# Attention: a pair's shift transposed once as 32 rows and laid into the query stack by two transfers on the chip

## The chip, the cores and the metric

The kernel runs on one NeuronCore of a Trainium2 chip. Its engines run beside each other and meet at semaphores: TensorE (PE: matmuls and transposes, results into PSUM), VectorE (DVE), ScalarE (ACT), GpSimd (POOL) and SyncE (SP, which issues DMA transfers here). The metric is the device time of one execution in microseconds (us).

## What is computed

Four layers on a stream `x` of 2 x 2048 tokens with 256 channels: linear attention, a mixture of experts, softmax attention on a hyperboloid, and a second mixture of experts. The change lies in the third one:

```python
x = L0_attn_x
x = x + _L0_attn_ref(_layernorm(x, axis=-1), ...)
x = x + _L0_ffn_ref(_layernorm(x, axis=-1), ...)
x = x + _L1_attn_ref(_layernorm(x, axis=-1), ...)
x = x + _L1_ffn_ref(_layernorm(x, axis=-1), ...)

# in _L1_attn_ref: B = 2, T = 2048, h = 16 heads of dh = 16
sc = (-jnp.einsum('bhqi,bhki->bhqk', q[..., :1], k[..., :1]) + jnp.einsum('bhqc,bhkc->bhqk', q[..., 1:], k[..., 1:])) / dh ** 0.5
at = jax.nn.softmax(sc, axis=-1)
out = jnp.einsum('bhqk,bhkc->bhqc', at, vv)
```

## The kernel before

The stages stand one behind the other with a barrier between them. Softmax attention is the stage `at` (function `attention`, tiles named `at_...`). It works on 16 pairs of heads (`NPAIR`: 8 pairs in each of 2 batches). The queries of a pair lie in `k.QT` (rows of `l1c_QT` in the profile): 64 partitions for each of the two heads, 2048 columns, one for each query, in float16. Keys lie in `k.KT` in the same way. A pair takes `ST` = 32 steps. A step is half of one key tile: two units of 128 keys x 1024 columns (512 queries of each head).

What sets the order is the order in which each engine's instructions are written, with waits on counting semaphores. There is no scheduler. In one step:

- PE does `scores(p, step, 0)` (L1581, two matmuls), `weigh` of the step two back (L1595, eight matmuls as the trace counts a step: each float32 one is recorded in two passes), `scores(p, step, 1)`, and one `means` (L1608).
- ACT does one exponential of 128 x 1024 for each unit (L1681), from `psS` into `pexp`. `psS` has two buffers, so `scores` of a unit waits until the exponential of two units before is done (`raised`).
- DVE takes the maximum of what `means` wrote (L1695), one for each step.

Softmax needs a shift for each query, so that the exponentials stay in range. The kernel estimates it: `means` multiplies the queries with sums of four keys, `reduce` takes the row maximum into a column of `mx`, and six steps ahead of the next pair all 32 columns are there (16 query tiles x 2 heads). `make_shift` (L1713 to L1716) turns `mx` into `shift`, 128 partitions x 32 float16. The shift must then lie along the columns of the query stack, as row `ROW` = 32 of each head's 64 partitions, where a constant key row picks it up in `scores`. That turn is done in two halves of 8 tiles, at steps 27 and 29 (`TURNS`):

- `turn_shift` (L1632) on PE: 16 transposes of one column each, 128x1 into 1x128, eight for each head, into `psX`;
- `put_shift` (L1723) on DVE: two copies of 1 x 1024 (one for each head) from `psX` into `k.QT`, then a count on `x_free`, which hands `psX` on.

PE waits for all four copies (`q_ready`) ahead of the pair's first `scores`. `psX` is one bank; the results of the pair before go through it too, at steps 3 and 5 (`turn_out`, L1640, four float32 transposes of 128x128, and `divide`, L1738 to L1742, on DVE). The dictionary `x_use` numbers these uses.

Ahead of the loop stands a prologue for pair 0: `first_means` (L1620) and `first_reduce` (L1700) for 16 tiles and 3 more, `make_shift(0)`, and both halves of the turn. The last pair has no successor and needs neither `means` nor a shift, so there are 15 turned shifts inside the loop and one in the prologue. From step 26 of the last but one pair (pair 14) on there are no `means` either.

Of the kernel before, what the change touches and what calls it, by code (L numbers as in the profile page):

```python
# [23 lines left out]
P = 128  # L24
# [1464 lines left out]
def attention(nc, k):  # L1489
# [17 lines left out]
    AHEAD = 6  # L1507
    TURNS = (ST - 5, ST - 3)
    with Stage(nc, "at") as s:
# [4 lines left out]
        sa, sb_ = s.sb("sa", [P, ST]), s.sb("sb", [P, ST])  # L1514
        shift = s.sb("shift", [P, ST, 1], F16)
        oT = s.sb("oT", [P, 2, BANK])
# [4 lines left out]
        psX = s.ps("psX", [P, BANK])  # L1521
        (scored, raised, weighed, v_ready, o_out, maxed, reduced, k_ready, q_ready, shifted, x_turned, x_free, chain,
         divided, start) = (
            s.sem(n) for n in ("scored", "raised", "weighed", "vready", "oout", "maxed", "reduced", "kready", "qready",
                               "shifted", "xturned", "xfree", "chain", "divided", "start"))

        def uses():
            order = [("shift", 0, 0), ("shift", 0, 1)]
            for p in range(NPAIR):
                if p:  # L1530
                    order += [("out", p - 1, 0), ("out", p - 1, 1)]
                if p + 1 < NPAIR:
                    order += [("shift", p + 1, 0), ("shift", p + 1, 1)]
            return {u: n for n, u in enumerate(order + [("out", NPAIR - 1, 0), ("out", NPAIR - 1, 1)])}
# [17 lines left out]
        with nc.Block() as block:  # L1552

            @block.gpsimd
            def _(pool):
# [11 lines left out]
                for p in range(2, NPAIR):  # L1567

                    pool.wait_ge(weighed, 6 + (p - 1) * ST * 2)
                    take_v(p)  # L1570

            @block.tensor
            def _(pe):
# [48 lines left out]

                def turn_shift(p, half):
                    pe.wait_ge(shifted, p + 1)
                    use = x_use["shift", p, half]
                    if use:
                        pe.wait_ge(x_free, use)
                    view = psX[:, :].bitcast(F16)
                    for hh in range(2):
                        row = hh * HR + ROW  # L1630
                        for n in range(KT16 // 2):
                            mm = pe.transpose(view[row:row + 1, n * P:(n + 1) * P],  # L1632
                                              shift[:, (half * (KT16 // 2) + n) * 2 + hh, :], k.identh[:, :])
                    mm.then_inc(x_turned, 1)

# [10 lines left out]
                for t in range(AHEAD // 2):  # L1646
                    first_means(1, t)
                for half in range(2):
                    turn_shift(0, half)

                pe.wait_ge(reduced, ST + AHEAD)
                for p in range(NPAIR):
                    pe.wait_ge(q_ready, 4 * (p + 1))
                    for step in range(ST):
                        scores(p, step, 0)
                        if step >= 2:
                            weigh(p, step - 2)
                        elif p:
                            weigh(p - 1, ST - 2 + step)
                        scores(p, step, 1)  # L1660
                        q, n = mean_at(p, step)
                        if q < NPAIR:
                            means(q, n)
                        if step in (3, 5) and p:
                            turn_out(p - 1, step // 4)
                        if step in TURNS and p + 1 < NPAIR:
                            turn_shift(p + 1, TURNS.index(step))
                weigh(NPAIR - 1, ST - 2)
# [16 lines left out]
            def _(dve):  # L1685
# [21 lines left out]
                def make_shift(p):  # L1707
                    dve.wait_ge(reduced, (p + 1) * ST)
                    if p:

                        dve.wait_ge(x_turned, x_use["shift", p - 1, 1] + 1)
                    q = 0.25 / (QS * QS)
                    link(p, 0, dve.tensor_scalar(sa[:, :], mx[:, :], q, 280.0, ALU.mult, ALU.add))  # L1713
                    link(p, 1, dve.tensor_scalar(sa[:, :], sa[:, :], -280.0, None, ALU.min))
                    link(p, 2, dve.scalar_tensor_tensor(sb_[:, :], mx[:, :], q, sa[:, :], ALU.mult, ALU.max))
                    dve.tensor_scalar(shift[:, :, 0], sb_[:, :], -QS * QS / KONE, None, ALU.mult).then_inc(shifted, 1)  # L1716

                def put_shift(p, half):
                    use = x_use["shift", p, half]
                    dve.wait_ge(x_turned, use + 1)  # L1720
                    for hh in range(2):
                        row = hh * HR + ROW
                        dve.tensor_copy(keys(k.QT, p)[row:row + 1, half * UN:(half + 1) * UN],  # L1723
                                        psX[:, :].bitcast(F16)[row:row + 1, :]).then_inc(q_ready, 1)
                    dve.wait_ge(q_ready, 4 * p + 2 * half + 2)
                    dve.sem_inc(x_free, 1)

# [25 lines left out]
                for t in range(AHEAD // 2):  # L1753
                    first_reduce(1, t)
                put_shift(0, 0)
                put_shift(0, 1)
                for p in range(NPAIR):
                    for step in range(ST):
# [10 lines left out]
                        if step in (3, 5) and p:  # L1769
                            divide(p - 1, step // 4)  # L1770
                        if step in TURNS and p + 1 < NPAIR:
                            put_shift(p + 1, TURNS.index(step))
                for y in range(2):
# [440 lines left out]
```

## Time and profile before

| | |
|---|---|
| median of 3 runs | 2600.14 us |
| lowest and highest | 2599.54, 2600.92 us |
| the profiled execution | 2600.85 us, its span 2599.0 us |
| mean granted TensorE clock | 0.938 |
| PE, DVE, ACT, POOL busy | 2240.9, 1263.2, 1492.3, 383.1 us |

Times in the profile count from the span's start. The attention stage runs in it from about 755 to 1790 us. An instruction's duration runs from its start to its end, and the next of the same engine may begin before that end. So the rate of an engine is read from the distance of two starts, called pitch below, and not from the durations. A row of the timeline gathers instructions of one kind as long as no idle time of 0.15 us or more lies between them; its second column runs from the first start to the last end.

### The profile page before, as it was taken

How to read it: one execution, taken by the hardware profiler on the slowest of the kernel's cores; microseconds unless marked ns; L12 is line 12 of the kernel's file. 1: busy time of each engine (PE TensorE's matmuls, PEld its weight loads, DVE VectorE, ACT ScalarE, POOL GpSimd, SP SyncE). 2: the span in 40 equal slices, each digit the busy share in tenths (PEclk: the TensorE clock that was granted, in tenths of full speed). 3: DMA queues.
4: the chain of work that ended last, by engine and by line, in shares of the span. 5: the costliest groups of instructions: out<-in, count | busy, mean ns of one | idle time of the engine just before them, and what ended most of it. 6: DMA issues, size and time to landing. Idle time of an engine off the chain costs nothing. (4 is left out here: it accounts for less than half of the span.)

```text
span 2599.0 us, 41169 instructions
## 1 busy us (share of the span) xinstructions
PE 2240.9 (86%) x12824; PEld 1055.9 (41%) x12825; DVE 1263.2 (49%) x2727; ACT 1492.3 (57%) x2466; POOL 383.1 (15%) x628
## 2 busy tenths in 40 slices
PE   4996799933979999999999999999057999999993
PEld 3783455522642222222222222225034666666662
DVE  5566522246884444444444444421465444444444
ACT  2213433224748999999999999997553222222220
POOL 0030266641000000000000000000001222222220
PEclk9998899976988999999999999999578999999996
DMA  5001122241100000000000000003263444344445
GB/s 180 1 1 65 45 77 79 75 176 69 34 9 1 1 1 1 1 1 1 1 1 1 1 1 1 1 1 115 80 183 99 119 119 119 119 120 120 120 116 211
DMA packets 105458, 160.19 MB, mean 62 GB/s; under 512 B 9465, under 2 KB 81905, under 8 KB 105329
## 3 DMA queue, kind: packets, MB, share of 16 engines
q1 hardware_dynamic: 90544, 117.05, 14.8%
q0 software_dynamic: 13632, 37.24, 4.4%
q10 hardware_dynamic: 1152, 4.19, 0.4%
q8 instruction: 79, 1.29, 0.2%
q14 instruction: 51, 0.41, 0.1%
HBM read 118.86 MB, written 35.39 MB: 59 GB/s over the span
## 5 line engine op out<-in xcount | busy, mean ns | idle before, releaser
L1681 ACT ACTIVATE at_pexp<-at_psS 128x1024 f32<-128x1024 f32 x1024 | 968.0, 1023 | 59.8 <-PE at_psS L1581 56.8
L1695 DVE TENSOR_REDUCE at_mx<-at_psM 128x1 f32<-128x512 f32 x474 | 327.4, 691 | 478.3 <-PE at_psM L1608 478.3
L1595 PE MATMUL at_psO<-at_pexp,at_vst 128*32 128x512 f32 x4096 | 546.4, 605 | 0.1
L1581 PE MATMUL at_psS<-l1c_QT,l1c_KT 64*128 64x512 f16 x2048 | 403.9, 387 | 12.2 <-ACT at_pexp L1681 6.1
L1581 PEld LDWEIGHTS at_psS<-l1c_QT,l1c_KT 64*128 64x128 f16 x2048 | 100.4, 92 | 617.0 <-ACT at_pexp L1681 556.0
L2008 PE MATMUL ex_psH<-wide_wgu,ex_xT 128*128 x852 | 339.9, 549 | 0.1
L2052 ACT ACTIVATE ex_sg<-ex_bias 128x228 f32<-128x228 f32 x213 | 83.7, 393 | 288.1 <-DVE ex_bias L2078 255.1
L2078 DVE TENSOR_TENSOR ex_bias<-ex_psH,ex_bias 128x456 f32<-128x456 f32 x213 | 134.7, 633 | 198.4 <-PE ex_psH L2008 192.9
L2008 PEld LDWEIGHTS ex_psH<-wide_wgu,ex_xT 128*128 128x128 f32 x852 | 157.2, 191 | 138.5 <-issue 138.4
L1005 POOL DMA_INDIRECT expert_rows<-ex_y,ex_odx x142 | 140.4, 989 | 397.4 <-issue 286.0
L2031 PE MATMUL ex_psY<-wide_w2b,ex_hT 114*128 (+1 forms) x852 | 196.0, 379 | 0.7 <-DVE ex_y L2097 0.7
L1608 PE MATMUL at_psM<-at_ksumT,l1c_QT 64*128 64x512 bf16 x474 | 179.1, 378 | 0.7
L2031 PEld LDWEIGHTS ex_psY<-wide_w2b,ex_hT 114*128 114x128 f32 (+1 forms) x852 | 156.3, 190 | 19.8 <-issue 1.3
L999 POOL DMA_INDIRECT ex_xg<-normed,ex_idx x142 | 139.7, 983 | 112.0 <-POOL ex_odx L990 53.5
L1061 PE MATMUL ex_psH<-l_w,ex_xT 128*128 x284 | 141.3, 621 | 5.6 <-issue 2.2
L1557 POOL COPY at_vst<-wide_x 128x512 f32<-128x512 f32 x16 | 9.7, 609 | 898.5 <-PE at_psO L1595 898.5
L1595 PEld LDWEIGHTS at_psO<-at_pexp,at_vst 128*32 128x32 f32 x4096 | 80.6, 108 | 130.2 <-issue 122.9
L1122 DVE TENSOR_SCALAR ex_y<-ex_psY,top_wgt 128x256 f32<-128x256 f32 x71 | 34.3, 483 | 176.6 <-DMA expert_rows<-ex_y,ex_odx 105.8
L2044 ACT ACTIVATE ex_xT<-ex_psX 128x256 f32<-128x256 f32 x71 | 27.2, 384 | 157.1 <-PE ex_psX L1997 157.1
L1099 ACT ACTIVATE ex_hT<-ex_psG 128x256 f32<-128x256 f32 x71 | 27.3, 384 | 131.6 <-PE ex_psG L1070 79.0
L985 POOL CAST ex_idx<-top_tok 128x1 uint32 (+1 forms) x142 | 28.6, 201 | 428.2 <-POOLq L74 420.4
L2083 DVE TENSOR_TENSOR ex_h<-ex_bias,ex_sg 128x228 f32<-128x228 f32 x213 | 82.8, 389 | 11.2 <-ACT ex_sg L2052 11.2
(337 smaller groups left out, 2631.5 us busy)
## 6 DMA issues: line engine op xcount, KB each, us to landing
ex_bias<-in_L_ffn_bg SPq DMA_DIRECT2D x71, 342.0 KB
ex_bias<-in_L_ffn_b SPq DMA_DIRECT2D x71, 342.0 KB
normed<-rt_area SPq DMA_DIRECT2D x16, 512.0 KB, 2.6
lm_y<-expert_rows SPq DMA_DIRECT2D x16, 512.0 KB
cb_y<-expert_rows SPq DMA_DIRECT2D x16, 512.0 KB, 7.6
w_raw<-in_L_ffn_w SPq DMA_DIRECT2D x24, 256.0 KB
wide_wgu<-in_L_ffn_Wg SPq DMA_DIRECT2D x8, 684.0 KB
wide_wgu<-in_L_ffn_W SPq DMA_DIRECT2D x8, 684.0 KB
```

Source lines behind the costliest of these rows:

```text
L999: pool.indirect_dma_start(xg[:, g, :], None, k.xn_d, bass.IndirectOffsetOnAxis(idx[:, g, :], 0)).then_inc(got[g], 16)
L1005: pool.indirect_dma_start(k.y_d, bass.IndirectOffsetOnAxis(odx[:, j, :], 0), y[:, j, :], None).then_inc(put[j], 16)
L1061: mm = pe.matmul(psH[:, j, :], xT[:, j, kk, :], k.w13[:, ds(e, 1), kk, :].rearrange("p a c -> p (a c)"), start=(kk == 0), stop=(kk == KC - 1))
L1581: mm = pe.matmul(psS[:, n, hh * BANK:(hh + 1) * BANK], keys(k.KT, p)[r, kt * P:(kt + 1) * P], keys(k.QT, p)[r, c * BANK:(c + 1) * BANK], s ...
L1595: mm = pe.matmul(psO[g * VW:(g + 1) * VW, y, :], vst[:, p % 2, hh, kt, :], pexp[:, (p * ST + step) % 3 * 2 + n, hh * BANK:(hh + 1) * BANK] ...
L1608: pe.matmul(psM[:, :], keys(k.QT, p)[r, t * P:(t + 1) * P], ksumT[r, p % 2, :], start=True, stop=True).then_inc(maxed, 1)
L1681: act.activation(pexp[:, u % 6, :], psS[:, u % 2, :], ACT.Exp, scale=D ** -0.5 / (QS * QS)).then_inc(raised, 1)
L1695: dve.tensor_reduce(mx[:, n:n + 1], psM[:, :], AX.X, ALU.max).then_inc(reduced, 1)
L2008: mm = pe.matmul(psH[:, n, 0:G2].rearrange("p (n c) -> p n c", n=2), xT[:, j, kk, :], k.wgu[:, ds(e, 1), kk, :, n * HW:(n + 1) * HW].rearr ...
L2031: mm = pe.matmul(psY[:, 0:C], hT[0:rows, j, g, :], k.w2b[0:rows, ds(e, 1), g, :].rearrange("p a c -> p (a c)"), start=(g == 0), stop=(g == ...
L2052: act.activation(sg[:, n, :], bias[:, st.slot(1, BR), n, 0, :], ACT.Silu).then_inc(gated, 1)
L2078: dve.tensor_tensor(hb, psH[:, n, 0:G2].rearrange("p (n c) -> p n c", n=2), hb, ALU.add).then_inc(added, 1)
```

## The change

`shift` is laid out head by head (`[P, 2, KT16]`), and the turn is one transpose of the whole tile: 128x32 in, 32x128 out, at one place, step 28 (`TURN`). DVE copies these 32 rows of 128 from `psX` into a new SBUF tile `shiftT`. Then SP, which had nothing to do in this stage, issues two DMA transfers from SBUF to SBUF for each pair: 16 rows of `shiftT` (256 bytes each) become one row of 2048 columns in `k.QT`. PE waits for both transfers (`shift_in`) ahead of the pair's first `scores`. Before it writes `shiftT` again, DVE waits for the transfers of the pair before. A pair's shift is now one use of `psX` instead of two.

```diff
-    TURNS = (ST - 5, ST - 3)
+    TURN = ST - 4
-        shift = s.sb("shift", [P, ST, 1], F16)
+        shift = s.sb("shift", [P, 2, KT16], F16)
+        shiftT = s.sb("shiftT", [ST, P], F16)
...
+            @block.sync
+            def _(sp):
+                for p in range(NPAIR):
+                    sp.wait_ge(x_free, x_use["shift", p, 0] + 1)
+                    for hh in range(2):
+                        row = hh * HR + ROW
+                        sp.dma_start(keys(k.QT, p)[row:row + 1, :].rearrange("a (t c) -> a t c", c=P),
+                                     shiftT[hh * KT16:(hh + 1) * KT16, :]).then_inc(shift_in, 16)
...
-                def turn_shift(p, half):
+                def turn_shift(p):
                     pe.wait_ge(shifted, p + 1)
-                    use = x_use["shift", p, half]
+                    use = x_use["shift", p, 0]
                     if use:
                         pe.wait_ge(x_free, use)
-                    view = psX[:, :].bitcast(F16)
-                    for hh in range(2):
-                        row = hh * HR + ROW
-                        for n in range(KT16 // 2):
-                            mm = pe.transpose(view[row:row + 1, n * P:(n + 1) * P],
-                                              shift[:, (half * (KT16 // 2) + n) * 2 + hh, :], k.identh[:, :])
-                    mm.then_inc(x_turned, 1)
+                    pe.transpose(psX[:, :].bitcast(F16)[0:ST, 0:P], shift[:, :, :].rearrange("p h t -> p (h t)"),
+                                 k.identh[:, :]).then_inc(x_turned, 1)
...
-                for half in range(2):
-                    turn_shift(0, half)
+                turn_shift(0)
...
-                    pe.wait_ge(q_ready, 4 * (p + 1))
+                    pe.wait_ge(shift_in, 32 * (p + 1))
...
-                        if step in TURNS and p + 1 < NPAIR:
-                            turn_shift(p + 1, TURNS.index(step))
+                        if step == TURN and p + 1 < NPAIR:
+                            turn_shift(p + 1)
...
-                    dve.tensor_scalar(shift[:, :, 0], sb_[:, :], -QS * QS / KONE, None, ALU.mult).then_inc(shifted, 1)
-
-                def put_shift(p, half):
-                    use = x_use["shift", p, half]
-                    dve.wait_ge(x_turned, use + 1)
-                    for hh in range(2):
-                        row = hh * HR + ROW
-                        dve.tensor_copy(keys(k.QT, p)[row:row + 1, half * UN:(half + 1) * UN],
-                                        psX[:, :].bitcast(F16)[row:row + 1, :]).then_inc(q_ready, 1)
-                    dve.wait_ge(q_ready, 4 * p + 2 * half + 2)
-                    dve.sem_inc(x_free, 1)
+                    dve.tensor_scalar(shift[:, :, :].rearrange("p h t -> p t h"),
+                                      sb_[:, :].rearrange("p (t h) -> p t h", h=2), -QS * QS / KONE, None, ALU.mult).then_inc(shifted, 1)
+
+                def put_shift(p):
+                    dve.wait_ge(x_turned, x_use["shift", p, 0] + 1)
+                    if p:
+
+                        dve.wait_ge(shift_in, 32 * p)
+                    dve.tensor_copy(shiftT[:, :], psX[:, :].bitcast(F16)[0:ST, 0:P]).then_inc(x_free, 1)
...
-                put_shift(0, 0)
-                put_shift(0, 1)
+                put_shift(0)
...
-                        if step in TURNS and p + 1 < NPAIR:
-                            put_shift(p + 1, TURNS.index(step))
+                        if step == TURN and p + 1 < NPAIR:
+                            put_shift(p + 1)
```

On PE, at steps 27 to 29 of pair 0, the program before stands thus (L1581 is `scores`, L1595 `weigh`, L1608 `means`, L1632 the turn):

```order
L1608 MATMUL at_psM<-at_ksumT,l1c_QT 128x512
L1632 MATMUL at_psX<-top_identh,at_shift 1x128 x16
L1581 MATMUL at_psS<-l1c_QT,l1c_KT 128x512 x2
L1595 MATMUL at_psO<-at_pexp,at_vst 32x512 x4
L1581 MATMUL at_psS<-l1c_QT,l1c_KT 128x512 x2
L1608 MATMUL at_psM<-at_ksumT,l1c_QT 128x512
L1581 MATMUL at_psS<-l1c_QT,l1c_KT 128x512 x2
L1595 MATMUL at_psO<-at_pexp,at_vst 32x512 x4
L1581 MATMUL at_psS<-l1c_QT,l1c_KT 128x512 x2
L1608 MATMUL at_psM<-at_ksumT,l1c_QT 128x512
L1632 MATMUL at_psX<-top_identh,at_shift 1x128 x16
```

On the same engine at step 28, the changed program (its lines are L1591, L1605, L1618, and L1638 for the turn):

```order
L1591 MATMUL at_psS<-l1c_QT,l1c_KT 128x512 x2
L1605 MATMUL at_psO<-at_pexp,at_vst 32x512 x4
L1591 MATMUL at_psS<-l1c_QT,l1c_KT 128x512 x2
L1618 MATMUL at_psM<-at_ksumT,l1c_QT 128x512
L1638 MATMUL at_psX<-top_identh,at_shift 32x128
L1591 MATMUL at_psS<-l1c_QT,l1c_KT 128x512 x2
```

Two blocks of 16 transposes, behind the `means` of steps 27 and 29, have become one transpose behind that of step 28.

On DVE, from the shift of the next pair on, before (L1695 is `reduce`, L1716 the end of `make_shift`, L1723 `put_shift`, L1733 `take_out`):

```order
L1716 TENSOR_SCALAR at_shift<-at_sb 128x32
L1695 TENSOR_REDUCE at_mx<-at_psM 128x1 x2
L1723 COPY l1c_QT<-at_psX 1x1024 x2
L1695 TENSOR_REDUCE at_mx<-at_psM 128x1 x2
L1723 COPY l1c_QT<-at_psX 1x1024 x2
L1695 TENSOR_REDUCE at_mx<-at_psM 128x1 x3
L1733 COPY at_oT<-at_psO 128x512 x2
```

And in the changed program, at the same place on DVE:

```order
L1720 TENSOR_SCALAR at_shift<-at_sb 128x16x2
L1699 TENSOR_REDUCE at_mx<-at_psM 128x1 x3
L1728 COPY at_shiftT<-at_psX 32x128
L1699 TENSOR_REDUCE at_mx<-at_psM 128x1 x4
L1735 COPY at_oT<-at_psO 128x512 x2
```

Four copies of one partition each have become one copy of 32 partitions, and what brought the row into `k.QT` now stands on SP.

## Rows read from the trace of the kernel before

**Rows 1.** The page: span, busy times, and the granted TensorE clock in 40 slices
```profile
span 2599.0 us, 41169 instructions
...
PE 2240.9 (86%) x12824; PEld 1055.9 (41%) x12825; DVE 1263.2 (49%) x2727; ACT 1492.3 (57%) x2466; POOL 383.1 (15%) x628
...
PEclk9998899976988999999999999999578999999996
```

**Rows 2.** Waits, 800 to 1780 us: waiter, awaited: us in total, times, longest
```profile
PEld at_psS L1581 <- ACT at_pexp L1681: 546.4, 820, 0.8
...
ACT at_pexp L1681 <- PE at_psS L1581: 23.8, 87, 0.3
```

**Rows 3.** Timeline of ACT: start, us covered, instructions xcount, [idle before <- releaser]
```profile
862.87 40.41 ACT L1681 ACTIVATE at_pexp<-at_psS 128x1024 f32<-128x1024 f32 x43 [0.29 <-PE at_psS L1581]
903.57 1.02 ACT L1681 ACTIVATE at_pexp<-at_psS 128x1024 f32<-128x1024 f32 x1 [0.28 <-PE at_psS L1581]
904.88 2.85 ACT L1681 ACTIVATE at_pexp<-at_psS 128x1024 f32<-128x1024 f32 x3 [0.29 <-PE at_psS L1581]
907.93 1.02 ACT L1681 ACTIVATE at_pexp<-at_psS 128x1024 f32<-128x1024 f32 x1 [0.19 <-PE at_psS L1581]
909.25 11.56 ACT L1681 ACTIVATE at_pexp<-at_psS 128x1024 f32<-128x1024 f32 x12 [0.29 <-PE at_psS L1581]
...
925.29 40.42 ACT L1681 ACTIVATE at_pexp<-at_psS 128x1024 f32<-128x1024 f32 x43 [0.29 <-PE at_psS L1581]
...
1674.27 41.37 ACT L1681 ACTIVATE at_pexp<-at_psS 128x1024 f32<-128x1024 f32 x44 [0.29 <-PE at_psS L1581]
...
1719.87 11.35 ACT L1681 ACTIVATE at_pexp<-at_psS 128x1024 f32<-128x1024 f32 x12 [0.17 <-PE at_psS L1581]
1731.51 51.53 ACT L1681 ACTIVATE at_pexp<-at_psS 128x1024 f32<-128x1024 f32 x55 [0.29 <-PE at_psS L1581]
```

**Rows 4.** Timeline of PE around the first turn of one pair (step 27)
```profile
902.06 0.38 PE L1608 MATMUL at_psM<-at_ksumT,l1c_QT 64*128 64x512 bf16 x1
902.37 0.83 PE L1632 MATMUL at_psX<-top_identh,at_shift 128*1 128x128 f16 x16
903.13 0.39 PE L1581 MATMUL at_psS<-l1c_QT,l1c_KT 64*128 64x512 f16 x2
903.45 1.07 PE L1595 MATMUL at_psO<-at_pexp,at_vst 128*32 128x512 f32 x8
...
905.20 1.07 PE L1595 MATMUL at_psO<-at_pexp,at_vst 128*32 128x512 f32 x8
```

**Rows 5.** Timeline of DVE in the same step
```profile
902.48 0.69 DVE L1695 TENSOR_REDUCE at_mx<-at_psM 128x1 f32<-128x512 f32 x1 [1.22 <-PE at_psM L1608]
```

**Rows 6.** Timelines of DVE, PE and ACT at the end of the prologue
```profile
781.80 1.41 DVE L1723 COPY l1c_QT<-at_psX 1x1024 f16<-1x1024 f16 x2
784.85 1.41 DVE L1723 COPY l1c_QT<-at_psX 1x1024 f16<-1x1024 f16 x2 [1.64 <-PE at_psX L1632]
```
```profile
783.41 1.40 PE L1632 MATMUL at_psX<-top_identh,at_shift 128*1 128x128 f16 x16 [3.58 <-DVEq L1726]
786.36 1.04 PE L1581 MATMUL at_psS<-l1c_QT,l1c_KT 64*128 64x512 f16 x4 [1.55 <-issue]
```
```profile
787.01 4.69 ACT L1681 ACTIVATE at_pexp<-at_psS 128x1024 f32<-128x1024 f32 x5 [31.76 <-PE at_psS L1581]
```

**Rows 7.** Windows: stretch, us, busy us (x) of PE, PEld, DVE, ACT, POOL, clock, DMA share, GB/s
```profile
792.00:793.00 1.00, 1.00 (x8) 0.28 (x5) 0.00 (x0) 0.03 (x1) 0.00 (x0) 0.50 0.05 16
793.00:794.00 1.00, 1.00 (x11) 0.16 (x8) 0.69 (x1) 1.00 (x2) 0.00 (x0) 0.97 0.00 0
```

**Rows 8.** SP's transfers of L1361 (SBUF to SBUF) and L1143: issue ns, landing us
```profile
L1361 SPq DMA_DIRECT2D sh_v<-wide_x x32: 485/486/601, 622.8 to 725.3; - x32
...
DMA to landing us min/median/max: 2.0/2.0/2.1
```
```profile
DMA to landing us min/median/max: 3.8/7.6/12.7
```

More of the change, by code:

```diff
@@ L1521, in attention @@
         psX = s.ps("psX", [P, BANK])
-        (scored, raised, weighed, v_ready, o_out, maxed, reduced, k_ready, q_ready, shifted, x_turned, x_free, chain,
+        (scored, raised, weighed, v_ready, o_out, maxed, reduced, k_ready, shift_in, shifted, x_turned, x_free, chain,
          divided, start) = (
-            s.sem(n) for n in ("scored", "raised", "weighed", "vready", "oout", "maxed", "reduced", "kready", "qready",
+            s.sem(n) for n in ("scored", "raised", "weighed", "vready", "oout", "maxed", "reduced", "kready", "shiftin",
                                "shifted", "xturned", "xfree", "chain", "divided", "start"))
         def uses():
-            order = [("shift", 0, 0), ("shift", 0, 1)]
+            order = [("shift", 0, 0)]
             for p in range(NPAIR):
@@ L1532, in uses @@
                 if p + 1 < NPAIR:
-                    order += [("shift", p + 1, 0), ("shift", p + 1, 1)]
+                    order += [("shift", p + 1, 0)]
             return {u: n for n, u in enumerate(order + [("out", NPAIR - 1, 0), ("out", NPAIR - 1, 1)])}
@@ L1709, in make_shift @@
                     if p:
-                        dve.wait_ge(x_turned, x_use["shift", p - 1, 1] + 1)
+                        dve.wait_ge(x_turned, x_use["shift", p - 1, 0] + 1)
                     q = 0.25 / (QS * QS)
```

## The prediction

> **What bounds the kernel now.** The page comes first, only to place the stage: the span is 2599.0 us, and the clock row reads 9 in every slice of the attention loop [rows 1]. The page's busy shares don't say what limits that loop, so the waits of 800 to 1780 us are read next. PE's weight loads of `scores` waited 820 times for the exponential, 546.4 us in total, while ACT waited 87 times for `scores`, 23.8 us in total and never over 0.3 us [rows 2]. So the exponentials on ACT set the pace, and PE is late only at few places. A gain has to come out of these 87 places, from the prologue, or not at all.
>
> The timeline of ACT shows where they are [rows 3]. In the last pair, which turns nothing behind step 5, 55 exponentials cover 51.53 us: a pitch of (51.53 - 1.02) / 54 = 0.935 us. In an ordinary pair 43 of them cover 40.41 us, a pitch of (40.41 - 1.02) / 42 = 0.938. That is the undisturbed pace, 1.87 us for a step of two. Then come four gaps in a row, ahead of 903.57, 904.88, 907.93 and 909.25, and two more up to 925.29. The first four stand behind the two turns of the shift, at steps 27 and 29; the other two stand behind `turn_out`. The whole repeats from 862.87 to 925.29, 62.42 us for 64 exponentials, and every pair from 1 to 13 has the same picture.
>
> **What the turns cost now.** From 862.87 to 909.25 there are 43 + 1 + 3 + 1 = 48 exponentials in 46.38 us [rows 3]. At 0.938 they would take 45.01, so the two turns cost 1.37 us on the path. A little of it is paid back: behind a gap ACT runs at (2.85 - 1.02) / 2 = 0.915 for three pitches [rows 3], which gives back 3 x 0.023 = 0.07. That leaves 1.30 for a pair. Fourteen of the fifteen turned shifts in the loop are of this kind (those made in pairs 0 to 13): 14 x 1.30 = 18.2 us. In pair 14, without `means` in its last steps, 44 + 4 = 48 exponentials run from 1674.27 to 1719.87, 45.60 us, so 0.59 lost. Together 18.8 us.
>
> The timeline of PE says why a turn costs what it does [rows 4]. The `means` starts at 902.06, the 16 transposes at 902.37, and the next `scores` at 903.13. Without a turn, when PE is behind and works without waiting, the distance from one `weigh` to the next is 905.20 - 903.45 = 1.75 us; of it 0.32 lies between `scores` and `weigh` (903.13 to 903.45), 1.00 in `weigh`, and the rest, 0.43, in the second `scores` and `means`, about half each. So some 0.20 us pass from `means` to the next `scores` without a turn, and 1.07 with one: a turn takes 0.87 us of PE. The step has 1.87 - 1.75 = 0.12 us of slack, and two turns, 1.74 us of PE, cost ACT 1.30: each turn has 0.22 absorbed, from this step and the next.
>
> **What the change removes and adds on PE.** Out go 32 transposes and one of two turns for each pair, in comes one transpose of 32 columns. The 16 transposes cover 0.83 us, and one of them lasts about 0.22, so their pitch is 0.61 / 15 = 0.04 and they make 0.65 of the 0.87; the other 0.22 are the waits and the change from one kind of matmul to another. The new turn is then 0.22 + 0.04 = 0.26 us of PE, against 0.22 absorbed: 0.04 us lost, times 15 gives 0.6 us. No row shows a transpose with 32 weight columns in this place. The bounds are nothing (all absorbed) and the cost of `turn_out`, four transposes of full width in float32: from 909.25 to 925.29 there are 16 exponentials in 16.04 us against 15.01, so 1.03 for two, 0.5 each [rows 3], or 7.5 us for 15. The new turn has one short float16 transpose and not four, so it is near the lower end; I take 0.6 us.
>
> **DVE.** Four copies of 0.7 us each (two of them in 1.41) [rows 6] go, one copy of 128 columns comes. DVE had waited 1.22 us ahead of `reduce` [rows 5], and no ACT gap is traced to it, so this is worth nothing by itself. The new wait for `x_turned` stands behind the `reduce` of step 28, which takes 0.69 us; the transpose is done by then. The wait for the transfers of the pair before is one whole pair old. Behind both stand only the `reduce` of step 29 and what follows, which `means` needs a step later.
>
> **SP and the two transfers.** SP has no other work in this stage, so nothing is queued behind its wait. What counts is whether the row lies in `k.QT` when PE starts the next pair. Put onto an undisturbed step with the times of rows 4 and 5: `reduce` ends at 902.48 + 0.69 = 903.17, the copy at about 903.4 (an estimate, from 0.69 for 512 columns), the first issue comes at 903.5. An issue occupies SP for 0.49 us and a transfer from SBUF to SBUF lands 2.0 us after its issue [rows 8], so the second lands at 903.5 + 0.5 + 2.0 = 906.0. The next pair's first `scores` is due three steps behind the `scores` that would follow at about 902.37: 902.37 + 3 x 1.87 = 907.98. There are 2.0 us to spare, and inside the loop the transfers cost nothing. The row's transfer is 128 KB in 1 KB pieces, the new one 4 KB in pieces of 256 bytes. I take the row's 2.0 us. Bounds are about the same 2.0 and the 7.6 us of a transfer of 512 KB from HBM [rows 8].
>
> The page "DMA: Bandwidth & Descriptors" of the Trainium skill, section Specifications, puts the least size for full rate at 512 bytes and says that below it the engine reads, modifies and writes. No row here has such a transfer by itself; by this rule the pieces would be slower than the row's, and if that doubled the whole 2.0 us, the loop would still hide it.
>
> **The prologue.** Here the shift is on the path from its making to the first `scores`. Before, DVE is held by `first_reduce` until 781.80, copies until 783.2, waits for the second half's transposes (PE at 783.41, because `psX` was taken), copies from 784.85 to 786.26, and PE starts at 786.36 [rows 6]. After: the copy from 781.80 to about 782.0, the first issue at 782.1, the second at 782.6, its landing at 784.6, PE at 784.7. That is 1.7 us sooner. But PE runs at a granted clock of 0.50 there, the level of 1.2 GHz, and goes to 2.4 GHz only at 793.0 [rows 7]. If the rise stays at that moment instead of moving with the work, 1.7 us more of the loop run at half clock, where PE sets the pace, and up to half of the gain, 0.85 us, is lost. Between 0.85 and 1.7 I take 1.3 us.
>
> **The sum.** 18.8 + 1.3 - 0.6 = 19.5 us less. The profiled execution took 2600.85 us, so it would become 2581.3. That execution is 0.7 above the median of 2600.14, and the median would become 2580.6. Everything behind the loop starts behind a barrier and moves along whole; its low-clock stretches (the 5, 7 and 8 behind the loop in the clock row [rows 1]) can fall a little differently against the work, for which I allow 2 us either way.
>
> **The rivals.**
>
> *The turn stays dear.* The fixed share of a turn, 0.22 by the split above, might be larger with another shape of weights, so that one turn costs ACT what a `turn_out` does, 0.5 us. Then 7.5 us go instead of 0.6, and the time is 2587.5. For it: the split of 0.87 rests on differences of 0.1 us. Against it: both kinds of turn cost about in proportion to the PE time they take. 8 in 100.
>
> *Small pieces are slow.* A landing after 4.0 us instead of 2.0 costs nothing in the loop (2.0 to spare) and 2.0 in the prologue: 2582.6. 6 in 100.
>
> *The transfers come too late, slower than before.* The place is PE's wait for `shift_in` at each pair's start; behind it stand `scores`, and so ACT. The price is the landing beyond 4.0 us, for each of 15 pairs. At 5.3 us the 1.3 us gained for a pair are gone, and from there on the kernel is slower. At the 7.6 us of a large load [rows 8] it would be 15 x 3.6 = 54 us in the loop and 5.6 in the prologue against 19.5: about 2640. Against it: no other transfer of the program is under way in this stage, and the row's transfers landed within 2.0 to 2.1 us. 4 in 100.
>
> *The change doesn't do what it says.* The four gaps would come from steps 27 to 30 themselves, not from the turn, and the time would stay near 2599. Against it: pair 15 has no turn there and no gap [rows 3]. 2 in 100.
>
> *The part behind the loop moves by more than 2 us*, in either direction, by the clock: 4 in 100.
>
> **How the numbers follow.** The forecast has 76 in 100 and lies between 2578 and 2583. With the slow pieces (2582.6) and the new turn's cost somewhat up its range, 2577.5 to 2585.5 leaves less than 2 in 10 out: the dear turn, the late transfers, the change without effect. A difference of 0.2% (5.2 us) is about what a measurement of this kernel can tell from none. Faster by more than that: the forecast, the dear turn, the slow pieces and most of the clock case, 0.94. Within it: the change without effect, 0.02. Slower: the late transfers, 0.04.
>
> **What would show it.** In the changed kernel's ACT timeline the four gaps at each pair's end are gone, one group of some 55 exponentials runs on from step 5 or so to the next pair's start at a pitch of 0.938, and a pair takes 61.1 us instead of 62.42. On PE, 0.25 us or so at most lie between `means` and `scores` of step 28 beyond the usual. Landing of the new transfers reads about 2 us, and PE has no wait for them but in the prologue, where the first exponential starts near 785.3 instead of 787.01. I am wrong if a new gap stands at each pair's start (late transfers), if a gap of 0.3 us stays at step 28 (the turn stays dear), or if the stage gets shorter and the rest longer.

## The result, and the profile after

The changed kernel takes 2579.19 us (median of 6 runs, 2577.47 to 2581.85), against 2600.53 for the kernel before in the same comparison. The ratio is 0.9919, with an interval of 0.9906 to 0.9932: 0.8% faster, 21.3 us. Forecast were 2580.6, and 19.5 us less. The profiled execution has a span of 2578.4 us, 20.6 less than before.

From the page of the changed kernel: span, busy times, and the granted clock in 40 slices, as in [rows 1].

```profile
span 2578.4 us, 40128 instructions
...
PE 2220.9 (86%) x12328; PEld 1033.4 (40%) x12329; DVE 1223.7 (47%) x2679; ACT 1488.6 (58%) x2466; POOL 382.7 (15%) x628
...
PEclk9998899976988999999999999999588999999996
```

DVE lost 40 us of busy time and PE 20, and the span 20.6. That the second pair of numbers agrees is no proof of a cause; the timeline of ACT has to show where the 20.6 lie. It stands here from the start of the attention loop on, in the columns of [rows 3] (the line of the exponential is now L1685):

```profile
783.64 4.69 ACT L1685 ACTIVATE at_pexp<-at_psS 128x1024 f32<-128x1024 f32 x5 [29.78 <-PE at_psS L1591]
789.61 1.94 ACT L1685 ACTIVATE at_pexp<-at_psS 128x1024 f32<-128x1024 f32 x2 [1.27 <-PE at_psS L1591]
792.48 62.20 ACT L1685 ACTIVATE at_pexp<-at_psS 128x1024 f32<-128x1024 f32 x66 [0.93 <-PE at_psS L1591]
854.97 3.89 ACT L1685 ACTIVATE at_pexp<-at_psS 128x1024 f32<-128x1024 f32 x4 [0.29 <-PE at_psS L1591]
...
859.16 56.63 ACT L1685 ACTIVATE at_pexp<-at_psS 128x1024 f32<-128x1024 f32 x60 [0.29 <-PE at_psS L1591]
916.08 3.89 ACT L1685 ACTIVATE at_pexp<-at_psS 128x1024 f32<-128x1024 f32 x4 [0.29 <-PE at_psS L1591]
920.26 56.63 ACT L1685 ACTIVATE at_pexp<-at_psS 128x1024 f32<-128x1024 f32 x60 [0.29 <-PE at_psS L1591]
```

The four gaps at a pair's end are gone, and 60 exponentials run in one group across the boundary of two pairs. A pair's 64 exponentials take 920.26 - 859.16 = 61.10 us, against 62.42 before [rows 3]. The two gaps that are left belong to `turn_out`.

PE and DVE at step 28, which [rows 4, 5] answer to (L1618 is `means`, L1638 the turn, L1591 `scores`, L1728 the copy, L1579 the two transfers):

```profile
900.18 0.38 PE L1618 MATMUL at_psM<-at_ksumT,l1c_QT 64*128 64x512 bf16 x1
...
900.48 0.23 PE L1638 MATMUL at_psX<-top_identh,at_shift 128*32 128x128 f16 x1
900.59 0.69 DVE L1699 TENSOR_REDUCE at_mx<-at_psM 128x1 f32<-128x512 f32 x1 [1.14 <-PE at_psM L1618]
...
900.64 0.39 PE L1591 MATMUL at_psS<-l1c_QT,l1c_KT 64*128 64x512 f16 x2
...
901.20 0.20 DVE L1728 COPY at_shiftT<-at_psX 32x128 f16<-32x128 f16 x1
901.43 1.14 SPq L1579 DMA_DIRECT2D l1c_QT<-at_shiftT  x2
...
906.31 0.39 PE L1591 MATMUL at_psS<-l1c_QT,l1c_KT 64*128 64x512 f16 x2
```

From `means` to the next `scores` it is 0.46 us now, 1.07 before. The last line is the next pair's first `scores`, four steps behind those of 898.63. The transfers read as follows (issue in ns on SP, then landing in us):

```profile
L1579 SPq DMA_DIRECT2D l1c_QT<-at_shiftT x32: 502/586/1326, 780.5 to 1695.6; - x32
...
DMA to landing us min/median/max: 1.6/1.7/2.6
```

The median landing is 1.7 us for 4 KB in pieces of 256 bytes, less than the 2.0 of 128 KB in pieces of 1 KB [rows 8]. The second transfer is issued at about 902.0 and lands at 903.7; the next pair's first `scores` starts at 906.31. The transfer has 2.6 us to spare.

### The profile page after: what moved, and what is told of

The parts are those of the page before. It is cut to its first block and busy times, and to the rows that moved or that the text cites. A ratio compares the mean times of both kernels' runs of the same rounds, so it can differ in the third digit from the quotient of the medians.

```text
span 2578.4 us, 40128 instructions
## 1 busy us (share of the span) xinstructions
PE 2220.9 (86%) x12328; PEld 1033.4 (40%) x12329; DVE 1223.7 (47%) x2679; ACT 1488.6 (58%) x2466; POOL 382.7 (15%) x628
## 5 line engine op out<-in xcount | busy, mean ns | idle before, releaser
L1685 ACT ACTIVATE at_pexp<-at_psS 128x1024 f32<-128x1024 f32 x1024 | 964.2, 1023 | 43.5 <-PE at_psS L1591 40.5
L1605 PE MATMUL at_psO<-at_pexp,at_vst 128*32 128x512 f32 x4096 | 547.1, 606 | 0.1
L1591 PE MATMUL at_psS<-l1c_QT,l1c_KT 64*128 64x512 f16 x2048 | 403.6, 387 | 14.5 <-issue 5.6
L1591 PEld LDWEIGHTS at_psS<-l1c_QT,l1c_KT 64*128 64x128 f16 x2048 | 99.4, 92 | 633.0 <-ACT at_pexp L1685 599.6
L1618 PE MATMUL at_psM<-at_ksumT,l1c_QT 64*128 64x512 bf16 x474 | 179.1, 378 | 0.7
L1605 PEld LDWEIGHTS at_psO<-at_pexp,at_vst 128*32 128x32 f32 x4096 | 80.6, 108 | 125.3 <-issue 124.3
```

The source lines that it names most:

```text
L1591: mm = pe.matmul(psS[:, n, hh * BANK:(hh + 1) * BANK], keys(k.KT, p)[r, kt * P:(kt + 1) * P], keys(k.QT, p)[r, c * BANK:(c + 1) * BANK], s ...
L1605: mm = pe.matmul(psO[g * VW:(g + 1) * VW, y, :], vst[:, p % 2, hh, kt, :], pexp[:, (p * ST + step) % 3 * 2 + n, hh * BANK:(hh + 1) * BANK] ...
L1618: pe.matmul(psM[:, :], keys(k.QT, p)[r, t * P:(t + 1) * P], ksumT[r, p % 2, :], start=True, stop=True).then_inc(maxed, 1)
L1685: act.activation(pexp[:, u % 6, :], psS[:, u % 2, :], ACT.Exp, scale=D ** -0.5 / (QS * QS)).then_inc(raised, 1)
```

## The experiments

**Which part of the turn cost the time.** Three kernels start from the kernel before and lighten one part of the turn inside the loop; the prologue is left alone. A fourth starts from the changed kernel and leaves the turn out, with its waits and counts fitted to that.

```diff
 # half_transposes: 8 instead of 16 in a turn (one_transpose: 1 for each head, 2 in a turn)
-                        for n in range(KT16 // 2):
+                        for n in range(4 if p else KT16 // 2):
...
-                        dve.tensor_copy(keys(k.QT, p)[row:row + 1, half * UN:(half + 1) * UN],
-                                        psX[:, :].bitcast(F16)[row:row + 1, :]).then_inc(q_ready, 1)
+                        n = 4 * P if p else UN
+                        dve.tensor_copy(keys(k.QT, p)[row:row + 1, half * UN:(half + 1) * UN].rearrange("a (r c) -> a r c", c=n),
+                                        psX[:, :].bitcast(F16)[row:row + 1, 0:n].unsqueeze(1).to_broadcast(
+                                            [1, UN // n, n])).then_inc(q_ready, 1)
```

```diff
 # short_copies
-                        dve.tensor_copy(keys(k.QT, p)[row:row + 1, half * UN:(half + 1) * UN],
-                                        psX[:, :].bitcast(F16)[row:row + 1, :]).then_inc(q_ready, 1)
+                        n = P if p else UN
+                        dve.tensor_copy(keys(k.QT, p)[row:row + 1, half * UN:half * UN + n],
+                                        psX[:, :].bitcast(F16)[row:row + 1, 0:n]).then_inc(q_ready, 1)
```

```diff
 # no_turn, from the changed kernel
-                for p in range(NPAIR):
+                for p in range(1):
                     sp.wait_ge(x_free, x_use["shift", p, 0] + 1)
...
-                        if step == TURN and p + 1 < NPAIR:
+                        if step == TURN and p + 1 < 1:
                             turn_shift(p + 1)
```

> The kernel before, with 8 instead of 16 transposes in each turn of the shift inside the loop (30 turns, for pairs 1 to 15); VectorE's copies keep their 1024 columns by reading the written 512 twice, so half of the shift is wrong. Theory PE (a turn costs what its TensorE time exceeds the slack of its step): a turn takes 0.87 - 8 x 0.04 = 0.55 us of TensorE, 0.22 of it is absorbed, so a pair loses 0.66 instead of 1.30: about 9.5 us less than before. Theory DVE (the four copies of 0.7 us hold up the reduction, and so the exponentials): no change. Theory of fixed cost (a turn costs by being there): no change or under 3 us.

> The kernel before, with 2 instead of 16 transposes (one for each head) in each turn of the shift inside the loop; the copies keep their 1024 columns by reading the same 128 eight times, so most of the shift is wrong. Theory PE: a turn takes 0.87 - 14 x 0.04 = 0.31 us of TensorE, 0.22 absorbed, so a pair loses about 0.18 instead of 1.30: 16 to 17 us less than before. Theory DVE: no change. Theory of fixed cost: under 5 us.

> The kernel before, with all its transposes, but inside the loop VectorE's four copies of a pair's shift take 128 of 1024 columns each, so most of the shift is left at zero. Theory PE: no change beyond 1 us, and a pair still takes 62.4 us. Theory DVE: 15 to 19 us less, a pair at about 61.1.

> The changed kernel with its turn, copy and transfers left out inside the loop (the prologue's stay), so the shift is wrong for pairs 1 to 15. It is the floor of what a turn can cost. Theory PE: the one transpose of 0.26 us against 0.22 absorbed costs 0.04 a pair, so 0 to 1 us less than the changed kernel (about 2578.5), and a pair goes from 61.11 to 61.0 or 61.1. Rival (the turn stays dear, at what one of the other transposes costs): 0.3 to 0.5 a pair, 5 to 7.5 us less. Rival (the wait for the transfers at each pair's start costs): the first distance of a pair, 1.00 us now, becomes 0.92.

| kernel | median us | ratio to before | a pair, us |
|---|---|---|---|
| before (13 runs beside these) | 2599.83 | 1 | 62.42 |
| short_copies | 2600.74 | 1.0004 (0.9994 to 1.0013) | 62.43 |
| half_transposes | 2586.28 | 0.9949 (0.9933 to 0.9966) | 61.56 |
| one_transpose | 2583.40 | 0.9940 (0.9923 to 0.9956) | 61.20 |
| changed (another comparison) | 2579.19 | 0.9919 (0.9906 to 0.9932) | 61.10 |
| no_turn | 2579.21 | 0.9921 (0.9904 to 0.9937) | 61.00 |

A pair's time is the distance of the two groups of exponentials that begin behind the second `turn_out`. These are the lines, two for each of `half_transposes`, `one_transpose`, `short_copies` and `no_turn`, in this order:

```profile
922.80 41.34 ACT L1681 ACTIVATE at_pexp<-at_psS 128x1024 f32<-128x1024 f32 x44 [0.29 <-PE at_psS L1581]
...
984.36 8.51 ACT L1681 ACTIVATE at_pexp<-at_psS 128x1024 f32<-128x1024 f32 x9 [0.29 <-PE at_psS L1581]
```
```profile
921.80 56.72 ACT L1681 ACTIVATE at_pexp<-at_psS 128x1024 f32<-128x1024 f32 x60 [0.29 <-PE at_psS L1581]
...
983.00 9.42 ACT L1681 ACTIVATE at_pexp<-at_psS 128x1024 f32<-128x1024 f32 x10 [0.29 <-PE at_psS L1581]
```
```profile
923.17 40.42 ACT L1681 ACTIVATE at_pexp<-at_psS 128x1024 f32<-128x1024 f32 x43 [0.29 <-PE at_psS L1581]
...
985.60 6.60 ACT L1681 ACTIVATE at_pexp<-at_psS 128x1024 f32<-128x1024 f32 x7 [0.29 <-PE at_psS L1581]
```
```profile
922.50 56.52 ACT L1683 ACTIVATE at_pexp<-at_psS 128x1024 f32<-128x1024 f32 x60 [0.29 <-PE at_psS L1589]
...
983.50 9.42 ACT L1683 ACTIVATE at_pexp<-at_psS 128x1024 f32<-128x1024 f32 x10 [0.29 <-PE at_psS L1589]
```

With short copies nothing moves, not even by 0.02 us in a pair. Two of them take 0.48 us instead of 1.41, so 1.9 of DVE's 2.8 us went from each pair, and those were hidden. With fewer transposes the pair gets shorter: the cost of the turn was TensorE's. It isn't a price for being there either, since `one_transpose`, with both turns in place, gives back 1.22 us of a pair. `no_turn` is the floor, 61.00 us. Above it stand 1.42 us with two turns of 16 transposes, 0.56 with two of 8, 0.20 with two of 2, and 0.10 with the one turn of the change. The new turn is thus nearly free, and the rival "the turn stays dear" is ruled out: all that is left to gain at this place is 15 x 0.10 = 1.5 us. The medians of `no_turn` and of the changed kernel don't show so little (2579.21 and 2579.19); the traces do, with 975.47 and 976.94 us from the first exponential to the last. The first distance of a pair, 1.00 us, is the same in both, so the wait for the transfers costs nothing there.

Halving brought more than was expected, 0.86 us for a pair and not 0.64. The PE timelines of `half_transposes` and of `one_transpose` say why:

```profile
904.38 0.38 PE L1608 MATMUL at_psM<-at_ksumT,l1c_QT 64*128 64x512 bf16 x1
904.68 0.40 PE L1632 MATMUL at_psX<-top_identh,at_shift 128*1 128x128 f16 x8
905.01 0.39 PE L1581 MATMUL at_psS<-l1c_QT,l1c_KT 64*128 64x512 f16 x2
```
```profile
903.55 0.38 PE L1608 MATMUL at_psM<-at_ksumT,l1c_QT 64*128 64x512 bf16 x1
903.85 0.22 PE L1632 MATMUL at_psX<-top_identh,at_shift 128*1 128x128 f16 x2
904.00 0.39 PE L1581 MATMUL at_psS<-l1c_QT,l1c_KT 64*128 64x512 f16 x2
```

The turn of 8 took 0.63 - 0.20 = 0.43 us of PE, not 0.55, and that of 2 took 0.45 - 0.20 = 0.25. With 0.87 for 16, the cost isn't a fixed share and an equal step for each transpose: two pass almost inside the fixed share, the next six cost 0.03 each, and the last eight 0.055 each. Why, these runs don't show. What they do show is what ACT loses. With two turns in a pair, one costs ACT on average (1.42 / 2) = 0.71 for 0.87 us of PE, (0.56 / 2) = 0.28 for 0.43, and 0.10 for 0.25; the one turn of the change costs 0.10 for 0.46 - 0.20 = 0.26. That is about 0.16 us less than the turn takes on PE. It is a mean over two places and no constant: put start by start against the exponentials of `no_turn`, the first turn of a pair costs 0.79, 0.36 and 0.18 us (16, 8 and 2 transposes) and the second 0.62, 0.19 and 0.01. The first has some 0.07 us absorbed, the second 0.25. Why they differ isn't shown.

**Whether the transfers are hidden, and by how much.** The changed kernel with its turn later:

```diff
-    TURN = ST - 4
+    TURN = ST - 2      # turn_at_30; ST - 1 in turn_at_31
```

> The changed kernel with its turn at step 30 instead of 28: two steps of 1.87 us later, 3.74 against 2.6 to spare, so the transfers land 1.1 us too late. Theory: 15 x 1.1 = 17 us more, about 2596, and a pair takes 62.2 us, nearly what it took before the change. Rival (buffers take it up): no change.

> The changed kernel with its turn at step 31, the last of a pair, instead of 28. In its trace the second transfer of a turn at step 28 lands at about 903.7 (issue 902.0, 1.7 to landing) and the next pair's first scores are due at about 906.3, so it has 2.6 us to spare. Three steps of 1.87 later it lands 3.0 us too late. Theory (the wait for the transfers is on the path by as much as they are late): 3.0 us for each of 15 pairs, 45 us more than the changed kernel, about 2624. Rival (buffers between TensorE and ScalarE take it up): under 15 us more.

`turn_at_30` took 2596.22 us, 17.0 more than the changed kernel, where 17 were expected. A pair takes 920.93 - 858.63 = 62.30 us. Its waits, 800 to 1780 us, name the transfers; all 15 pairs wait for them now:

```profile
PEld at_psS L1591 <- DMA l1c_QT<-at_shiftT: 24.6, 15, 1.7
...
PE at_psS L1591 <- DMA l1c_QT<-at_shiftT: 17.4, 15, 1.2
```

Each is late by 17.4 / 15 = 1.2 us, which fits the 2.6 to spare at step 28 and shows that no buffer takes it up. So the turn at step 28 hides its transfers completely, and two steps later the change would have given back four fifths of its gain.

`turn_at_31` took 2652.69 us, 2% slower than before (ratio 1.0201, 1.0184 to 1.0218), and 73.5 more than the changed kernel instead of the 45 expected. Its 15 waits are about as long as foreseen, 46.2 us in all, but more follows them. Here are these waits (800 to 1830 us), and its PE timeline and windows (columns of [rows 7]) at one pair's start:

```profile
PE at_psS L1591 <- DMA l1c_QT<-at_shiftT: 46.2, 15, 3.9
```
```profile
915.75 0.61 PE L1591 MATMUL at_psS<-l1c_QT,l1c_KT 64*128 64x512 f16 x2 [3.86 <-DMA l1c_QT<-at_shiftT]
916.28 1.93 PE L1605 MATMUL at_psO<-at_pexp,at_vst 128*32 128x512 f32 x8
...
919.24 1.07 PE L1605 MATMUL at_psO<-at_pexp,at_vst 128*32 128x512 f32 x8
```
```profile
912.00:914.00 2.00, 0.00 (x0) 0.00 (x0) 0.57 (x2) 0.58 (x1) 0.00 (x0) 1.00 0.04 10
914.00:916.00 2.00, 0.25 (x2) 0.10 (x2) 0.00 (x0) 0.00 (x0) 0.00 (x0) 0.87 0.02 2
...
915.50:915.75 0.25, 0.00 (x1) 0.01 (x2) 0.00 (x0) 0.00 (x0) 0.00 (x0) 0.50 0.00 0
...
916.00:918.00 2.00, 2.00 (x10) 0.20 (x8) 0.00 (x0) 1.03 (x1) 0.00 (x0) 0.50 0.00 0
918.00:920.00 2.00, 2.00 (x17) 0.44 (x13) 0.86 (x2) 1.20 (x2) 0.00 (x0) 0.78 0.00 0
920.00:922.00 2.00, 2.00 (x17) 0.37 (x13) 1.67 (x3) 2.00 (x3) 0.61 (x1) 1.00 0.00 0
```

PE stands idle for 3.9 us, the longest of the 15 waits. The granted clock is down at 0.50 (1.2 GHz) a quarter of a us before PE has work again at 915.75, and a `weigh` takes 1.93 us instead of 1.07 until it is back at 2.4 GHz. From the first `scores` to the second `weigh` PE takes 919.24 - 915.75 = 3.49 us, where at full clock it is 0.32 + 1.75 = 2.07 (the distances of [rows 4]): 1.4 us lost. The other 14 waits last 2.6 to 3.4 us, and the clock fell at each. In nine of the 15 pairs it had fallen when the first `scores` began (they last 0.61 us, as above); in the other six these still last 0.39, and it fell up to 1.4 us after the work had begun again. So a late transfer costs its lateness, and after these longer waits a stretch at half clock on top: (73.5 - 46.2) / 15 = 1.8 us are left for each pair. With the 1.2 us of `turn_at_30` the clock did not fall; it reads 1.00 all through that loop. The slow rival of the prediction was priced too low by this part.

**The prologue.** `old_prologue` is the changed kernel with pair 0's shift turned as before, by 32 transposes in two rounds and four copies (`turn_first` and `put_first` are the old `turn_shift` and `put_shift`, for pair 0 alone):

```diff
-                turn_shift(0)
+                for half in range(2):
+                    turn_first(half)
...
-                put_shift(0)
+                put_first(0)
+                put_first(1)
```

> The changed kernel with pair 0's shift turned as before, by 32 transposes in two rounds and four copies straight into the query stack. In the two traces the first exponential came 8.63 us (before) and 6.58 us (changed) behind the end of the tile of the shift. Theory (the transfers shorten the prologue by 2.05 us, and the granted clock, which does not rise sooner, takes half of it back): 8.6 us to the first exponential, pair 0 one us shorter, and 1.0 us more in all. Rival (the whole prologue counts): 2.0 us more in all. Rival (upstream scatter, the prologue gives nothing): no change from the shift to the end of pair 0.

From the start of the instruction that writes `shift` (778.20, 776.82 and 777.14 us before, in the changed kernel and here) the first exponential came after 8.81, 6.82 and 8.81 us. Up to the first gap of `turn_out` in pair 1 it took 80.48, 78.15 and 79.20 us. The lines of `old_prologue`:

```profile
785.95 4.69 ACT L1703 ACTIVATE at_pexp<-at_psS 128x1024 f32<-128x1024 f32 x5 [31.77 <-PE at_psS L1591]
...
856.34 3.89 ACT L1703 ACTIVATE at_pexp<-at_psS 128x1024 f32<-128x1024 f32 x4 [0.29 <-PE at_psS L1591]
```

So the transfers bring the first exponential 1.99 us forward, and 79.20 - 78.15 = 1.05 us of that remains. The median, 2581.87, is 2.7 above the changed kernel's and can't tell 1 from 2 us; the distances can. They hardly scatter: up to the 55th exponential of pair 0, ahead of its first turn, it took 59.50 to 59.63 us in the six traces whose prologue has the two transfers and nothing else new, and 60.66 to 60.81 in the five with the old one. The rest goes where PE runs at half clock. In the changed kernel:

```profile
790.00:791.00 1.00, 1.00 (x5) 0.20 (x8) 0.69 (x1) 1.00 (x2) 0.00 (x0) 0.50 0.00 0
791.00:792.00 1.00, 1.00 (x8) 0.00 (x0) 0.00 (x0) 0.55 (x1) 0.00 (x0) 0.59 0.00 0
792.00:793.00 1.00, 1.00 (x13) 0.37 (x13) 0.31 (x1) 0.52 (x1) 0.00 (x0) 1.00 0.00 0
```

The clock rises at about 791.8, 15.0 us behind the writing of `shift`; before it was 793.0, 14.8 behind, and in `old_prologue` 792.1, 15.0 behind. Exponentials that start 2.0 us sooner get the full clock no sooner, so 2.0 us more of the loop run at half clock.

**Keeping PE busy while the transfers fly.** If the clock follows what PE did before, work without a use in the prologue's wait should lift it.

```diff
                 turn_shift(0)
+                for n in range(12):
+                    pe.matmul(psM[:, :], k.identh[:, :], keys(k.KT, 0)[:, (n % 4) * BANK:(n % 4 + 1) * BANK],
+                              start=True, stop=True)
```

```diff
 # warm_one_transfer: the same, with waits for 16 instead of 32 for each pair, and
-                    for hh in range(2):
-                        row = hh * HR + ROW
-                        sp.dma_start(keys(k.QT, p)[row:row + 1, :].rearrange("a (t c) -> a t c", c=P),
-                                     shiftT[hh * KT16:(hh + 1) * KT16, :]).then_inc(shift_in, 16)
+                    sp.dma_start(keys(k.QT, p)[ROW:ROW + HR + 1:HR, :].rearrange("a (t c) -> a t c", c=P),
+                                 shiftT[:, :]).then_inc(shift_in, 16)
```

> The changed kernel with twelve extra matmuls of 128x512 float16 behind the prologue's turn, into a PSUM bank that nothing reads until it is written again; they fill the 5.6 us in which TensorE waits for the transfers. In six traces the granted clock rose 14.5 to 15.0 us behind the end of the tile of the shift, wherever the first scores stood. Theory (what TensorE does ahead of the first scores lifts the clock, and the low clock costs pair 0 of the changed kernel 2 us): the clock rises before the first exponential or within 3 us of it, pair 0 takes 60.2 to 61.2 us instead of 62.3, and 1 to 2 us go in all. Rival (the clock does not follow this work): the rise stays near 14.7 us behind the shift, and nothing changes.

> The same, and a pair's two rows laid by one transfer instead of two. Theory: SyncE's second issue, 0.5 to 0.6 us, goes from the prologue's chain, so the first exponential comes 6.0 us behind the shift instead of 6.6; with the clock up, this counts in full: 0.6 us less than with two transfers, about 2 us less than the changed kernel in all. In the loop nothing changes, since the transfers have 2.6 us to spare there. Rival (one transfer of twice the rows lands later by as much): no difference to two.

The windows of `warm_prologue` around the first exponential (783.02 us):

```profile
777.00:781.00 4.00, 4.00 (x10) 1.41 (x11) 3.10 (x4) 0.00 (x0) 0.00 (x0) 0.50 0.00 0
782.00:783.00 1.00, 0.41 (x4) 0.24 (x5) 0.00 (x0) 0.00 (x0) 0.00 (x0) 1.00 0.03 4
784.00:785.00 1.00, 0.39 (x2) 0.10 (x2) 0.13 (x1) 1.00 (x3) 0.00 (x0) 0.82 0.00 0
787.00:788.00 1.00, 1.00 (x8) 0.00 (x0) 0.00 (x0) 0.71 (x1) 0.00 (x0) 0.50 0.00 0
788.00:789.00 1.00, 1.00 (x13) 0.23 (x9) 0.13 (x1) 0.34 (x1) 0.00 (x0) 0.97 0.00 0
```

The clock rose before the first exponential, fell again in the two steps without `weigh`, where PE mostly waits for ACT (0.39 busy in the row of 784), and rose for good at about 788.0, 11.6 us behind the writing of `shift` (776.41) and not 15.0. From the writing of `shift` (776.41 and 775.99) to the first gap of `turn_out` in pair 1 it took 853.08 - 776.41 = 76.67 us, and 852.28 - 775.99 = 76.29 with one transfer: 1.5 and 1.9 us less than the 78.15 of the changed kernel. With one transfer the first exponential came 6.10 us behind the writing and not 6.61, 0.5 sooner as expected; of that 0.4 remained. The medians, 2577.01 (0.9914, 0.9900 to 0.9927) and 2575.87 (0.9910, 0.9896 to 0.9923), are the lowest of all, though their intervals overlap the changed kernel's 0.9919. `warm_one_transfer` is the version I would keep.

**Two that did not help.** `spread_out` is the changed kernel with the eight transposes of a pair's result one to a step, and `plain_turn` does the turn by an ordinary matmul.

```diff
 # spread_out
+    OUTS = (3, 4, 5, 6, 12, 13, 14, 15)
...
-                        if step in (3, 5) and p:
-                            turn_out(p - 1, step // 4)
+                        if step in OUTS and p:
+                            n = OUTS.index(step)
+                            turn_out(p - 1, n // 4, range(n % 4, n % 4 + 1))
```

```diff
 # plain_turn
-                    pe.transpose(psX[:, :].bitcast(F16)[0:ST, 0:P], shift[:, :, :].rearrange("p h t -> p (h t)"),
-                                 k.identh[:, :]).then_inc(x_turned, 1)
+                    pe.matmul(psX[0:ST, 0:P], shift[:, :, :].rearrange("p h t -> p (h t)"), k.identh[:, :],
+                              start=True, stop=True).then_inc(x_turned, 1)
```

> The changed kernel with the other transposes of a pair, the eight of its result (four at step 3, four at step 5), spread one to a step over steps 3 to 6 and 12 to 15. Theory (a step absorbs about 0.2 us of TensorE, and what is over is lost): a block of four took 0.66 us and cost 0.5, two of them 1.05 a pair. One float32 transpose takes about 0.15 us, with its waits up to 0.3, so a pair loses at most 0.2 instead of 1.05: 60.2 to 60.4 us instead of 61.11, 12 to 14 us less than the changed kernel, about 2566. Rival (the cost is the change from one kind of matmul to another, which now comes eight times): no gain, or a loss.

> The changed kernel with its turn as an ordinary matmul of the shift with the identity (float32 result) instead of a transpose instruction. It measures the fixed 0.22 us of a turn by itself. Theory of the transpose mode (going into it and out of it costs): the distance from means to scores at step 28 falls from 0.46 to 0.25 us, and a pair from 61.11 to 61.01. Rival (the waits or the start behind means cost, whatever the instruction): 0.46 and 61.1 stay.

`spread_out` took 2594.25 us, 15 more than the changed kernel instead of 13 less. Its PE timeline at one of the eight steps:

```profile
916.92 0.38 PE L1619 MATMUL at_psM<-at_ksumT,l1c_QT 64*128 64x512 bf16 x1
917.23 0.33 PE L1647 MATMUL at_psX<-top_ident,at_oT 128*128 128x128 f32 x1
917.49 0.39 PE L1592 MATMUL at_psS<-l1c_QT,l1c_KT 64*128 64x512 f16 x2
```

One transpose alone takes 917.49 - 916.92 - 0.20 = 0.37 us of PE. ACT's groups in those steps begin at 917.13, 919.24 and 921.35, 2.11 apart and not 1.87, so each loses 0.24: only 0.13 us are absorbed, the slack of its own step (0.12 in the prediction), since the next step has a transpose too. Eight of them lose 1.9 us, where the two blocks of four lost 1.05, and a pair takes 979.29 - 917.13 = 62.16 us. I had taken 0.3 us at most for one, and 0.2 absorbed as if every step had that for itself. It came out as the rival said, with a price for each time that another kind of matmul comes in.

`plain_turn` shows that the price isn't one of the transpose mode. It took 2578.61 us, a pair in it 981.23 - 920.11 = 61.12, and at step 28 it reads

```profile
900.02 0.38 PE L1618 MATMUL at_psM<-at_ksumT,l1c_QT 64*128 64x512 bf16 x1
...
900.49 0.39 PE L1591 MATMUL at_psS<-l1c_QT,l1c_KT 64*128 64x512 f16 x2
```

with the matmul at 900.33, 0.31 us behind `means`, and `scores` 0.47 behind it. One small instruction between `means` and `scores` costs some 0.2 us beyond its own work, transpose or not; what that is stays open.

## Why the prediction was right

- **What bounds the loop** held. ACT sets the pace, and PE's turns at steps 27 and 29 made its gaps; `short_copies` and `half_transposes` show it by lightening one and the other. A side remark of the prediction was misread: the clock row does not say 9 in every slice of the loop. The first slice, 780 to 845 us, says 8, from the half clock up to 793.0.
- **1.30 us for a pair, 18.8 in all**: measured 62.42 - 61.10 = 1.32 net of the new turn's cost, so 1.42 for what was removed. The 0.1 more stands at the start of the next pair, whose first distance is 1.11 us before and 1.00 in the changed kernel and in `no_turn`: the 0.07 that the prediction took off as paid back is lost again there.
- **The new turn, 0.26 us of PE, 0.04 lost**: the 0.26 came out exactly (0.46 - 0.20), though the split it was made from, 0.04 for each transpose, did not hold for 8 of them. The loss was 0.10, because 0.16 is absorbed and not 0.22. This takes back half of the point before: 1.32 net for a pair, where the sum has 1.26.
- **DVE for nothing, the transfers hidden**: both shown, DVE's part for the 1.9 of 2.8 us that `short_copies` took away. To spare are 2.6 us, where I had 2.0. The rival of the small pieces did not come true. The page "DMA: Bandwidth & Descriptors" of the Trainium skill, section Specifications, lets one expect a loss below 512 bytes. None is seen in the 1.7 us to landing of these 256-byte pieces; but the 2.0 us beside it are those of a transfer with 32 times the bytes, and no run here changes the size of the pieces alone.
- **The prologue, 1.3 us**: the first exponential came 2.0 us sooner (I had 1.7), the clock took half of it back (I had up to half), and 1.05 stayed.
- **The stage in sum**: from the writing of `shift` to the first gap of pair 1, 80.48 - 78.15 = 2.33 us; then 1.31 for each of 13 pairs, 17.0; and 0.7 from there to the last exponential, for pair 14, where the prediction had 0.59. That makes 20.0 us, against the forecast of 19.5. The spans differ by 20.6, but not by these 20.0 and a small rest: the changed kernel's trace writes `shift` 1.4 us earlier, ahead of anything that was changed, and takes 0.9 us longer behind the last exponential. The runs of one kernel differ by 4 us (2577.47 to 2581.85), so neither of these, nor the 1.4 us between forecast and median, can be laid to a cause. That the total came within 1.4 us is in part luck; the 20.0 of the stage is what bears the prediction out.

## What to carry to other kernels

In this kernel an engine off the critical path cost nothing as long as its detour fitted into the slack of the steps it fell in. So count a detour on the pacing chain as its time on the engine less that slack, once for each detour; many short ones can cost more than one long one (1.9 us against 1.05 here). A transfer that replaces copies was free as long as it landed before its reader: measure the time to spare and leave the issue early, for being late costs the lateness in full, and more if TensorE's clock falls. Filling TensorE's wait ahead of a busy loop can be worth more than shortening the wait (1.5 us against 1.05 here).

## What was not expected of the hardware

- After 2.6 to 3.9 us without work at a pair's start the granted clock fell to 0.50, in nine of 15 cases before the work had begun again and in six up to 1.4 us after; after 1.2 us it did not fall. The fall cost about 1.8 us each time.
- A transfer of 16 pieces of 256 bytes from 16 partitions into one partition landed in 1.7 us, and occupied SP's issue for 0.50 to 0.59 us, no less than the 0.49 of a transfer of 128 KB [rows 8].
- One more instruction of PE between `means` and `scores`, transpose or ordinary matmul, took 0.26 to 0.27 us of PE. Two transposes of one column took 0.25, eight 0.43 and sixteen 0.87.
